# Small VectorE steps with constants read from memory columns, and another order of steps on every engine

## What is computed

```
def fp4_quant_dequant(x):                     # blocks of 16 along the last dim
    scale = max(abs(xb)) / 6.0
    scale = maximum(scale, 1e-12)
    q = GRID[searchsorted(MID, abs(xb / scale))] * sign(xb) * scale

def _ln(x, g, b):
    return (x - mean(x)) / sqrt(var(x) + 1e-05) * g + b

v = x @ v_w + v_b; scores = kernel(i - j) + q_mod + k_mod + MIX * q.k / sqrt(8), causal
ctx = softmax(scores) @ v
h = _ln(x + ctx @ out_w + out_b, ln1_g, ln1_b)
s = _ln(h + gelu(h @ ffn_w1 + b1) @ ffn_w2 + b2, ln2_g, ln2_b)
f = fp4_linear(silu(fp4_linear(x, w_gate)) * fp4_linear(x, w_up), w_down)
```

## Time and profile before

| | us |
|---|---|
| median of 3 runs | 1921.82 |
| lowest, highest | 1917.81, 1922.19 |
| span of the profiled execution | 1916.1 |
| busy PE / DVE / POOL / ACT in it | 1822.3 / 1590.4 / 1095.4 / 930.2 |

### The profile page before, as it was taken

One profiled execution on the slowest core, in us unless ns is written; L12 is line 12 of the kernel. 1 busy time (PEld: TensorE's weight loads), 2 busy tenths in 40 slices (PEclk: granted clock), 3 DMA queues, 4 the chain that ended last, 5 costly groups with the idle time before them and its releaser, 6 DMA issues.

```text
span 1916.1 us, 37547 instructions
## 1 busy us (share of the span) xinstructions
PE 1822.3 (95%) x12803; PEld 1311.7 (68%) x12803; DVE 1590.4 (83%) x5143; ACT 930.2 (49%) x1939; POOL 1095.4 (57%) x797
## 2 busy tenths in 40 slices
PE   7888999999999999999999999999999999999987
PEld 3335677777767767676776767677776767677766
DVE  6788899788888989888888978888897988888863
ACT  3635454544546354544635454453645445463542
POOL 2446657465556647464665746565664756466562
PEclk8999999999999999999999999999999999999999
DMA  5534233232322233232223323233222333322211
GB/s 156 165 96 114 64 91 83 75 110 75 99 75 79 76 82 115 75 90 73 91 74 93 93 75 110 64 102 79 83 77 75 110 84 91 75 85 74 61 57 34
DMA packets 138646, 166.69 MB, mean 87 GB/s; under 512 B 19757, under 2 KB 100654, under 8 KB 138452
## 3 DMA queue, kind: packets, MB, share of 16 engines
q1 hardware_dynamic: 138458, 164.30, 30.5%
HBM read 127.85 MB, written 36.41 MB: 86 GB/s over the span
## 4 chain that ended last, share of the span: by engine, by line
PE 50%; DVE 26%; issue 12%; POOL 4%; DMA 3%; ACT 3%; SPq 2%; DVEq 0%; POOLq 0%; ACTq 0%
PE ps L760 8%; PE ps L769 7%; PE ps L701 7%; PE ps L718 4%; DVE Pr L1067 3%; PE ps L624 3%; PE ps L597 3%; PE ps L733 3%; PE ps L658 3%; PE ps L674 2%; DVE nmax L1037 2%; POOL slot L1215 2%; PE ps L654 2%; DMA Tz<-kernel_rows 2%; DVE st L958 2%
## 5 line engine op out<-in xcount | busy, mean ns | idle before, releaser
L1176 POOL TENSOR_TENSOR Pr<-Pr,Tz 128x768 f32<-128x768 f32 (+2 forms) x384 | 477.6, 1273 | 233.8 <-ACT Pr L833 230.0
L1037 DVE CUSTOM_DVE_ANT_0 ps<-ps,future 128x512 f32<-128x512 f32 (+3 forms) x1024 | 474.5, 516 | 52.9 <-issue 51.8
L833 ACT ACTIVATE Pr<-ps 128x384 f32<-128x384 f32 x512 | 243.1, 489 | 345.2 <-PE ps L658 343.9
L760 PE MATMUL ps<-catT,w 128*128 128x256 f32 x1024 | 237.8, 380 | 0.7 <-ACT catT L896 0.7
L769 PE MATMUL ps<-w,gT 128*128 128x256 f32 x1024 | 232.9, 381 | 0.9 <-ACT gT L913 0.9
L624 PE MATMUL ps<-KS,QS 108*128 108x512 bf16 (+3 forms) x1024 | 215.0, 300 | 17.9 <-DVE nmax L1037 13.2
L822 ACT ACTIVATE ps<-ps 128x512 f32<-128x512 f32 x256 | 150.5, 588 | 137.7 <-PE ps L654 136.1
L1067 DVE SCALAR_TENSOR_TENSOR Pr<-ps,Tz 128x512 f32<-128x512 f32 x256 | 175.3, 685 | 46.2 <-ACT ps L822 41.0
L769 PEld LDWEIGHTS ps<-w,gT 128*128 128x128 f32 x1024 | 190.8, 190 | 25.7 <-ACT gT L913 1.3
L760 PEld LDWEIGHTS ps<-catT,w 128*128 128x128 f32 x1024 | 189.6, 190 | 26.2 <-ACT catT L896 0.9
L718 PE MATMUL ps<-wdT,hqT 128*128 128x256 f32 x768 | 179.5, 383 | 0.7 <-ACT hqT L872 0.7
(11 more groups left out here) (239 smaller groups left out, 3270.0 us busy)
## 6 DMA issues: line engine op xcount, KB each, us to landing
Tz<-kernel_rows SPq DMA_DIRECT2D x256, 256.0 KB, 3.6
KS<-k_parts SPq DMA_DIRECT2D x32, 384.0 KB
QS<-q_parts SPq DMA_DIRECT2D x64, 192.0 KB
hY<-in_x SPq DMA_DIRECT2D x19, 512.0 KB, 5.1
xn<-in_x SPq DMA_DIRECT2D x17, 512.0 KB, 3.8
out<-y SPq DMA_DIRECT2D x15, 512.0 KB, 2.9
q_parts<-q_sp SPq DMA_DIRECT2D x16, 384.0 KB, 3.0
k_parts<-k_sp SPq DMA_DIRECT2D x16, 384.0 KB, 2.4
```

The lines of the kernel that those rows point to most:

```text
L760: ins = mm(dst[:, i * n:(i + 1) * n], w1[:, c, f * P:(f + 1) * P], catT[:, c, hf * n:(hf + 1) * n], start=c == 0, stop=c == KD - 1)
L833: inc(af(Pr[:, p % 4, e, at:at + wd], src[:, 0:wd], ACT.Exp), "a_exp")
L1037: ins = v.tensor_tensor_reduce(o, o, future[:, S - n:S], -1.0, 3e38, ALU.add, ALU.min, nmax[:, 2 * pl + e, it:it + 1])
L1176: ins = g.tensor_tensor(a, a, Tz[:, p % 2, :, P * j:P * j + PAST[j]], ALU.mult)
```

## The change

Five constants (1, 1/6, 1e-12, `TIES_DOWN`, `EPS`) are put into columns of a new tile `consts` by five `memset`s at the start of the program (`N_MEMSETS` grows with them). `fp4_scales`, `layernorm_statistics` and `mfin` then take their scalars from these columns, one value per partition, in place of immediates; the copies of L961 and L1050 become a `tensor_scalar` that multiplies by one twice. The prologue's own statistics and weight scales, and the wide rounding steps (L934, L936), keep their immediates.

```
+        CONSTS = [1.0, 1.0 / 6.0, 1e-12, TIES_DOWN, EPS]
+        consts = sb("consts", [P, len(CONSTS)])
+        one, sixth, least, ties, eps = (consts[:, i:i + 1] for i in range(len(CONSTS)))
...
-                inc(v.tensor_scalar(sc[:, 1, :], sc[:, 0, :], 1.0 / 6.0, 1e-12, ALU.mult, ALU.max), name)
+                inc(v.tensor_scalar(sc[:, 1, :], sc[:, 0, :], sixth, least, ALU.mult, ALU.max), name)
...
-                inc(v.tensor_scalar(sc[:, 3, :], sc[:, 2, :], TIES_DOWN, None, ALU.mult), name)
+                inc(v.tensor_scalar(sc[:, 3, :], sc[:, 2, :], ties, one, ALU.mult, ALU.mult), name)
...
-                v.tensor_copy(ve[:, tt], st[:, tt, 0])
+                v.tensor_scalar(ve[:, tt], st[:, tt, 0], one, one, ALU.mult, ALU.mult)
...
-                inc(v.tensor_scalar(ve[:, tt], mv[:, tt, 1], EPS, None, ALU.add), "v_ve")
+                inc(v.tensor_scalar(ve[:, tt], mv[:, tt, 1], eps, one, ALU.add, ALU.mult), "v_ve")
...
-                    inc(v.tensor_copy(sh_sp[:, :, 0, :], nm), "v_m")
+                    inc(v.tensor_scalar(sh_sp[:, :, 0, :], nm, one, one, ALU.mult, ALU.mult), "v_m")
...
-        N_MEMSETS = 9
+        N_MEMSETS = 9 + len(CONSTS)
...
+                for i, c in enumerate(CONSTS):
+                    v.memset(consts[:, i:i + 1], c).then_inc(L["zero"], 1)
```

All lists of `ORDER` are written in another order. Of the `mid` lists, the whole of SP's and POOL's:

```
-            T.0 load.1 T.1 T.2 xload T.3 mio.1 T.4 splitio T.5 load.0 T.6 T.7 fin mio.0
+            T.0 load.1 T.1 xload T.2 T.3 T.4 mio.1 splitio T.5 load.0 T.6 T.7 fin mio.0
...
-            ln1 mul.0 lnb1 xnb mul.1 hq.0 mul.2 hr.0 projm.0 mul.3 hq.1 projm.1 hr.1 projm.2 xq xr mul.4 hq.2 mul.5
-            ln2 hr.2 fin mul.6 hq.3 mul.7 hr.3
+            xnb ln1 lnb1 mul.0 mul.1 mul.2 hq.0 hq.1 hr.0 projm.0 mul.3 projm.1 xq projm.2 hr.1 mul.4 hq.2 xr mul.5 hr.2
+            ln2 fin mul.6 hq.3 mul.7 hr.3
```

`psum_plan` now runs through all batches in turn, so the B ring, with its odd number of uses, alternates its banks from batch to batch and never takes the same bank twice running at a batch's border:

```
+    uses = [(at, u) for p, at in TURNS for w, s in orders[p] for u in kinds(s) for at in [at if p == "mid" else PARTS[p][w]]]
+    ahead = sum(len(kinds(s)) for w, s in orders["head"])
...
+        bank = banks[(i - ahead) % len(banks)]
+        place[at, u] = bank
+        if bank in last:
+            before[at, u] = last[bank]
+        last[bank] = (u, at)
```

## The result

The changed kernel takes 2000.43 us (median of 4 runs, 1999.29 to 2003.35) against 1922.01: a ratio of 1.041, interval 1.039 to 1.0429. It is slower by 78 us where I had forecast 25 us faster, and it lies outside the range. The executed span grew from 1916.1 to 1999.4 us; that is more than 78, because each of the four executions lasts 1.8 to 1.9 us longer than its own span, so that the profiled execution of before was, by this, one of its short ones. Ratios and intervals are of fast executions alone: now and then one is much slower, of whatever kernel (at most 4762.69 us), and the medians count it.

A forecast was written before the change was run, and what follows sets the result against it. TensorE (PE) was taken to bound the repeated batches. The span, 1916.1 - 22.4 (periods) - 2.5 (end) + 0 (head) = 1891.2 us, plus 5.7 gave 1897 us; range 1872 to 1921 us.

The forecast's parts named there:

- Do they still wait with scalars read from memory?: VectorE's small steps: with column scalars they would not wait for GpSimd, as L995's 64 runs lay between 397 and 414 ns.
- The price of the new forms: VectorE's small steps with columns: 194 ns on 44 columns, 214 on 64, 182 on 32, 154 on 4; 5.0 us saved a period.
- Each of its steps can only come earlier, the order being equal.: Repeated batch: with 5.0 us taken off VectorE, its steps come no later, so TensorE's waits for them shrink.
- The repeated batch, -1.6 us: Fourteen periods: 1.6 of the 2.0 us of removable TensorE waits go in each, 22.4 us in all.
- `lnb1` early: Repeated batch: `lnb1` ahead of a `silu` and a maximum, so the transposes at L750, waiting 0.3 us, find their input ready.
- `projm.2`: Repeated batch: ahead of the second `hr` on GpSimd, one or two us earlier, so the DMA late by 0.67 us starts earlier.
- The bound: Middle of the run: TensorE binds it, so only its idle time, 2.73 us a period, and hardly more can be won.
- The end, -2.5 us: Last batch: slow copy and companion fall from 2.40 to 0.31 us, 2 us of wait go, perhaps a half elsewhere; tail unchanged.
- The head: Start of the run: a 0.8 us loss and possible further wait set against saved first-batch waits; 0, 8 us either way.
- The 5.7 us between span and median: Whole run: measured runs stand 5.7 us above the profiled span, so this was added to the forecast span of 1891.2 us.
- (a): Rival, VectorE's small steps: columns bring nothing, they wait as before, and only the order works; 1917 us, chance 0.08.
- (c): Rival, GpSimd's queue: `projm.2` ends later, `T.5` lands later and `muld` holds TensorE; +10 us, 1932 us, chance 0.08.

The follow-up runs named there:

- price table: A program without the computation, timing VectorE forms with GpSimd idle, beside a product and beside a memset: 202 ns with column scalars against 122 with immediates on 44 columns.
- e7: The changed kernel with immediates again in the two scale steps alone: 1978.04 us, ratio 1.0293, batch 113.87 us.
- e5: The kernel before, in its own order, with the small VectorE steps as a one-element maximum or scalar_tensor_tensor: 1920.73 us, ratio 0.9991.
- e10: The kernel before plus four 128x1024 memsets on VectorE ahead of catT's exponent step in each batch: 2007.32 us, ratio 1.0441.
- e14: The kernel before with the changed lists for the last batch and tail alone, the changed bank plan and immediates: 1917.39 us, ratio 0.9982.
- e11: The changed order with immediates, with the first third of the repeated batch put back as before on all engines: 2008.33 us, ratio 1.046.
- e15: The changed lists with immediates, middle and last third of the repeated batch as before, only its first third changed: 1943.82 us, ratio 1.0107.

## Why the prediction was wrong, step by step

- **"Do they still wait with scalars read from memory?"** The step that failed first. I read 64 durations without spread as a form that does not wait, with the argument that GpSimd is busy more than half of the time. The share says nothing of the moments at which L995 ran; its neighbours in the timeline would have. GpSimd was idle or about to finish at all 64; beside a product of 2.8 us the same form lasts 2964 ns in the changed kernel. I also read 407 ns for 256 columns as the slow rate; it is the fast rate and fixed costs, as the price table shows.
- **The price of the new forms.** 194 ns on 44 columns were forecast, 304 is the least; 154 on 4 columns, where the changed kernel needs 286 at least. The lower bound, "the 186 of the fastest old one", left no room for a form that costs more than the old. VectorE, -5.0 us a batch forecast: +0.8 by the columns alone. What it costs the kernel by itself is small (+5.6 us); what a gain of 5.0 us would have been worth, no run shows, since none freed VectorE in the order of before.
- **"Each of its steps can only come earlier, the order being equal."** This is the step that cost most. The order was not equal, and this sentence covered it: the order alone is worth +51.6 us. I followed the queues (who waits for a semaphore behind whom) at two places and never laid GpSimd's instructions beside VectorE's in the new order, though the case's own rows showed what happens when they meet. That two-input steps meet GpSimd as well could be seen in no row: in the kernel of before all 64 of L941's slot additions took 891 to 894 ns. It is stated in the section of the Trainium skill that I cited for the copies.
- **The repeated batch, -1.6 us.** It is +5.7: +0.35 by columns, +3.87 by the order, +1.47 by the two meeting, which e7 places in the scale steps. Of the two gains that I had named, `lnb1` early did what I said at its place (TensorE's wait at the transposes L750 is gone from the list) and brought nothing that shows in the period; `projm.2` is not early at all: it starts 57.7 us into the batch (1105.02 in the changed kernel) and stood at 56.2 before.
- **The bound.** "What can be won there is PE's idle time" was not put to the test: the forms of e5 left VectorE as busy as before. And it bounds gains only. On the side of losses I had 0 to +1 us a batch; e10 shows that at VectorE's full stretch a microsecond of its work costs at least one, and the 15.6 us of idle time, which I called some slack, are elsewhere.
- **The end, -2.5 us.** In the changed kernel the two stretches are 0.7 us shorter than before; with immediates, compared at the same clock, 1.65. The cause forecast did not come: the slow copy and its companion last 1.49 and 0.90 us there, as before, and TensorE waits 0.80 and 0.84 us behind them. The gain is in the rest, for which I had forecast none. **The head**, 0 with 8 either way: +4.5, inside the bounds, though the heads of these kernels differ by as much with the same lists, so that this says little.
- **The 5.7 us between span and median.** They set one execution's span beside the median of others; execution by execution the difference is 1.8 to 1.9 us. That shifts the sum by some 4 us and changes nothing in the outcome. The bank change, costed at nothing, cost nothing in e14's repeated batch.
- **Rivals.** The mechanism of (a), the small steps wait as before, is what happened. Its price, 1917, was not: it put the columns at nothing and the order at a gain. It had 0.08, too little for a rule that only a misread row spoke against. (c) had the sign, but not its cause: VectorE's wait of 0.67 us for that DMA is gone from the changed kernel's period. The rival that was missing is GpSimd's products beside VectorE's steps, and with it the range's upper end.

## What to carry to other kernels

Before moving a step on one of two engines that block each other inside instructions, lay the two timelines side by side: idle time of the one may be what keeps the other fast, and filling it is no gain. A duration without spread proves that an instruction does not wait only if the other engine was in the middle of something when it started. And in an order written by hand, test a part of the order on all engines at once, since one engine's list put back alone measures how badly lists of two orders fit (here 78 and 134 us over the changed order, itself the slower one, part of it TensorE's clock); where a wait goes and the time stays, look for the next bound before dropping the suspect. Compare stretches only at the same granted clock: 1.7 us of a last batch, and of most batches of e10, were TensorE's clock and no engine's order.

## What the runs showed of the hardware that I had not expected

- VectorE and GpSimd do not meet only at semaphores, as I wrote ahead of the prediction. Who comes second waits until the other's instruction ends, and 0.25 us decide it: VectorE 0.10 us ahead gives 0.89, 0.15 us behind gives 2.42.
- Two column scalars cost 80 ns where the step is free, and nothing where it waits for GpSimd anyway (2094 to 2097 against 2095 and 2098 ns).
- VectorE's two-input forms in SBUF wait beside a GpSimd product but not beside its `memset` (L44); forms with one source in PSUM wait beside neither (L48, L50).
- GpSimd pays in turn: its subtraction of 704 columns (L1205) has a mean of 1778 ns in both runs with the new order, 1683 before; the product that VectorE's addition beat by 0.10 us lasts 2.46 us, where one that came first (at 1098.62) took 1.81.
- In some batches of the changed kernel the granted clock fell from 2.4 to 1.2 GHz behind TensorE's 1.04 and 0.68 us waits. One microsecond of it (columns as in the earlier trace rows, the clock is third from the end):

```profile
1128.00:1129.00 1.00, 1.00 (x20) 0.73 (x16) 0.96 (x6) 0.00 (x0) 0.92 (x2) 0.50 0.89 186
```

It cost nothing: batches with and without it are all 115.5 us long, and TensorE is idle 6.3 us in those with it and 7.3 in those without. I take VectorE to be the bound there. In e10, e11 and e15's last batch, by contrast, such 3.4 us cost 1.2 to 1.7.
